# Graph-attention layer: each head's context is stored by ScalarE's queue in place of SyncE's

## The reference

```python
q, k, v = (split_heads(x @ w + b) for each of wq, wk, wv)
scores = einsum("bhqd,bhkd->bhqk", q, k) * dh ** -0.5 + adj[:, None]
ctx = einsum("bhij,bhjd->bhid", softmax(scores), v)      # to [b, n, 384]
x1 = rmsnorm(x + ctx @ wo + bo, alpha1, gamma1)
ff = silu(x1 @ w1 + b1) @ w2 + b2
x2 = rmsnorm(x1 + ff, alpha2, gamma2)
out = layernorm(x + x2)
```

## Time and profile before

| | |
|---|---|
| median of 3 runs | 1932.65 us (1932.32 to 1933.24) |
| the profiled execution, its own time | 1933.91 us |
| its span in the trace | 1932.1 us |
| mean granted TensorE clock | 0.993 of full speed |
| PE busy | 1893.6 us, 98% |
| DVE busy | 1332.8 us, 69% |
| ACT busy | 1141.9 us, 59% |
| POOL busy | 1127.9 us, 58% |
| attention phase | to about 1008 us of the span |
| one batch of it in the loop | 60.2 us |

### The profile page before, as it was taken

How to read it: one execution, slowest core, us unless ns; L and a number is a source line. 1 busy time by engine, 2 the same in 40 slices (tenths; PEclk the granted TensorE clock), 3 DMA queues, 4 the chain that set the end, 5 groups by cost and what they waited for, 6 DMA issues and landing times. The chain is left out here.

```text
span 1932.1 us, 39573 instructions
## 1 busy us (share of the span) xinstructions
PE 1893.6 (98%) x10336; PEld 1608.8 (83%) x10336; DVE 1332.8 (69%) x2579; ACT 1141.9 (59%) x2056; POOL 1127.9 (58%) x1739
## 2 busy tenths in 40 slices
PE   6999999999999999999989999999999999999998
PEld 5777777777877777777768999999999999999997
DVE  5777777777777777777876666656656655666645
ACT  3777777777787777777765444334444334444432
POOL 3655445654456544555667566667665766655643
PEclk9999999999999999999989999999999999999999
DMA  5545545555444554565533222112222112222001
GB/s 173 152 142 152 160 124 142 143 151 160 123 143 142 151 158 125 146 176 152 154 115 125 88 87 84 50 43 83 87 87 87 54 41 79 87 87 87 28 31 41
DMA packets 118732, 214.36 MB, mean 111 GB/s; under 512 B 19489, under 2 KB 47905, under 8 KB 116769
## 3 DMA queue, kind: packets, MB, share of 16 engines
q1 hardware_dynamic: 118688, 213.87, 36.3%
HBM read 108.93 MB, written 41.94 MB: 78 GB/s over the span
## 5 line engine op out<-in xcount | busy, mean ns | idle before, releaser
L982 DVE TENSOR_TENSOR pT_lo<-ps_t,pT_hi 128x512 fp32r<-128x512 f32 x512 | 348.9, 687 | 104.1 <-ACT pT_hi L780 102.9
L780 ACT ACTIVATE pT_hi<-ps_t 128x512 fp32r<-128x512 f32 x512 | 303.1, 596 | 153.4 <-PE ps_t L1221 145.1
L773 ACT ACTIVATE probs<-probs,neg_max 128x512 f32<-128x512 f32 x512 | 357.0, 721 | 34.5 <-DVE neg_max L975 33.4
L975 DVE CUSTOM_DVE_ANT_0 probs<-ps_s,adj_s 128x512 f32<-128x512 f32 x448 | 294.3, 683 | 58.8 <-issue 27.3
L1221 PE MATMUL ps_t<-ident,probs 128*128 128x128 f32 x2048 | 314.2, 277 | 12.3 <-DVE pT_lo L982 9.6
L1221 PEld LDWEIGHTS ps_t<-ident,probs 128*128 128x128 f32 x2048 | 243.1, 141 | 97.4 <-issue 40.5
L1715 DVE TENSOR_TENSOR h_lo<-hidden,h_hi 128x512 fp32r<-128x512 f32 x192 | 170.2, 887 | 172.4 <-ACT h_hi L1625 172.2
L651 POOL CAST tails<-k_wide 16x512 fp32r<-16x512 f32 x384 | 233.4, 608 | 50.6
L647 POOL CAST k_wide<-k_wide 32x512 fp32r<-32x512 f32 x128 | 78.2, 611 | 315.2 <-DMA k_wide<-weights_hi 291.5
L1814 PE MATMUL ps_y<-w_hi,h_hi 128*128 128x384 f32 x768 | 258.2, 336 | 0.0
L1814 PE MATMUL ps_y<-w_hi,h_lo 128*128 128x384 f32 x768 | 257.0, 335 | 0.0
(11 more groups left out here) (114 smaller groups left out, 3963.2 us busy)
## 6 DMA issues: line engine op xcount, KB each, us to landing
ctx_dram<-ctx_stage SPq DMA_DIRECT2D x128, 224.0 KB
ctx_raw<-ctx_dram SPq DMA_DIRECT2D x15, 1792.0 KB, 7.3
q_wide<-weights_lo SPq DMA_DIRECT2D x192, 96.0 KB, 2.3
k_wide<-weights_hi SPq DMA_DIRECT2D x192, 96.0 KB, 2.4
adj_first<-in_adj SPq DMA_DIRECT2D x32, 512.0 KB, 6.5
adj_s<-in_adj SPq DMA_DIRECT2D x32, 512.0 KB, 6.4
rows<-in_xT SPq DMA_DIRECT2D x16, 768.0 KB, 4.9
rows<-in_x SPq DMA_DIRECT2D x16, 768.0 KB, 6.2
```

The costliest lines, as they stand in the source:

```text
L773: nc.scalar.activation(probs[:, at, :], probs[:, at, :], ACT.Exp, scale=-1.0, bias=neg_max[:, at:at + 1]).then_inc(exp_done, 1)
L780: nc.scalar.activation(pT_hi[:, h % 2, qt, :, :], ps_t[qt % 2][:, :].rearrange("p (k i) -> p k i", k=TT), ACT.Copy)\
L975: nc.vector.tensor_tensor_reduce(out=probs[:, at, :], in0=ps_s[qt][:, :], in1=rows, scale=-1.0, scalar=BIG, op0=ALU.add, op1=ALU.min, accu ...
L982: nc.vector.tensor_tensor(pT_lo[:, h % 2, qt, :, :].rearrange("p k i -> p (k i)"), ps_t[qt % 2][:, :], pT_hi[:, h % 2, qt, :, :].rearrange ...
```

## The change

`store_context` is called by ACT, right behind the staging copy of the same head, and no longer by SP. It waits for `ctx_staged` as before, which now is a wait of ACT for its own copy. All eight calls in SP's batch, and the two for heads 6 and 7 of the last batch, are gone. One wait is new on POOL: `last_batch` first waits until every projection of q and k is computed, before it writes W1 over the projection weights.

```diff
-    def store_context(self, sp, ctx_dram, b, h):
-        sp.wait_ge(self.ctx_staged, H * b + h + 1)
-        sp.dma_start(ctx_dram[b, h * ROWS:(h + 1) * ROWS, :, :].rearrange("r k n -> k r n"),
+    def store_context(self, act, ctx_dram, b, h):
+        act.wait_ge(self.ctx_staged, H * b + h + 1)
+        act.dma_start(ctx_dram[b, h * ROWS:(h + 1) * ROWS, :, :].rearrange("r k n -> k r n"),
                      self.ctx_stage[0:V_COLS, h % 2, :]).then_inc(self.ctx_stored[h % 2], DMA)
@@ SP, batch(b)
-                if not first:
-                    shared.store_context(sp, ctx_dram, b - 1, 6)
...
-                shared.store_context(sp, ctx_dram, b, 0)
...
                 stack_next("q", 1)
-                shared.store_context(sp, ctx_dram, b, 4)
 
                 if not last:
                     load_adj_pair(b + 1, 0)
                     load_adj_pair(b + 1, 1)
                 else:
                     seam(6)
-                shared.store_context(sp, ctx_dram, b, 5)
                 stack_next("k", 1)
@@ POOL, last_batch()
+                pool.wait_ge(proj_ready, 2 * KT * B)
                 split_w1(0)
@@ ACT, stage_context(b, h)
                 nc.scalar.activation(ctx_stage[0:V_COLS, h % 2, :], ps_g[bank][0:V_COLS, :], ACT.Copy)\
                   .then_inc(ctx_staged, 1)
+                shared.store_context(act, ctx_dram, b, h)
@@ SP, feed-forward phase
-            shared.store_context(sp, ctx_dram, LAST, H - 1)
```

More of the change, by code:

```diff
@@ L538, in batch @@
                     load_xT(b + 1)
-                if not first:
-                    shared.store_context(sp, ctx_dram, b - 1, 7)
                 if not last:
@@ L557, in batch @@
                     seam(2)
-                shared.store_context(sp, ctx_dram, b, 0)
                 if last:
                     seam(3)
-                shared.store_context(sp, ctx_dram, b, 1)
                 if last_but_two:
                     load_first_context(1)
-                shared.store_context(sp, ctx_dram, b, 2)
                 if last:
@@ L575, in batch @@
                     shared.load_x1_rows(sp, x, 0)
-                shared.store_context(sp, ctx_dram, b, 3)
                 if last_but_two:
@@ L619, in _ @@
             batch(LAST, last=True)
-            shared.store_context(sp, ctx_dram, LAST, 6)
         @block.gpsimd
```

## The result

| | before | after |
|---|---|---|
| median, us (range) | 1932.95 (1932.32 to 1933.69, 4 runs) | 1970.63 (1969.46 to 1971.53, 4 runs) |
| profiled execution: span, us | 1932.1 | 1967.7 |
| one batch in the middle, us | 60.21 | 62.45 |

The ratio is 1.0194, with a 95% interval from 1.0179 to 1.0209. The kernel became slower by 37.7 us, and 17.7 were forecast (1950.4 against 1932.65): the sign was right, the range of 1935 to 1972 just held it, and the loss is more than twice the forecast one.

What follows compares the result with a forecast made beforehand. PE was taken as the bound, busy 59.83 of 60 us per batch; 15 × (0.57 at head 2 + 0.46 at head 5) + 2.2 in batch 15 = 17.7 us, so 1932.65 becomes 1950.4 us, range 1935 to 1972.

Steps and rivals of the forecast that it cites:

- What is removed: SP loses 128 stores, 109 us of its time; PE waits for no DMA, so the gain was put at 0.
- G = 1.1: ACT's delay per store in us: overlap 0.11, wait 0.09, issue 0.85, restart 0.05; ends 0 or about 0.5, and 1.7.
- Head 2: Worst place: ACT's store delays q's high part, then DVE's low part and `pT_lo`; PE stands 0.57 us per batch.
- G = 1.4: A larger ACT delay per store: 1.16 us at head 2, 0.46 + 0.3 at head 5, 32 us in all.
- Head 5: ACT's late `pT_hi` delays DVE's `pT_lo`: PE stands 0.16 us, plus 0.3 waiting for SP's issues, 0.46 per batch.
- The stacking of q starts 1.4 us later: Listed under what costs nothing: q's stacking is delayed, but its readers on POOL stand idle for longer.
- Heads 0, 1, 3, 4, 6, 7: 0: At these heads the nearest `pT_lo` or bank keeps 0.1 to 0.6 us to spare, so the stores cost PE 0.
- Sum: 15 batches of 0.57 + 0.46 us give 15.5, plus 2.2 in batch 15: 17.7 us slower.
- Rival 1: The issue on ACT is hidden or short, under 0.8 us per store, and ACT's idle absorbs it: 1932 to 1936 us; chance 0.15.
- Rival 2: Two issuers hinder each other at every store, about 1.7 us each: 47 us slower, 1980; chance 0.07 together with rival 4.
- Rival 3: Faster: freed SP starts loads and stores sooner, ending at most 7.5 us of PE's waits: 1925 us; chance 0.05.
- Rival 4: PE's standing drops its clock, 2 us lost per batch: 1980 us; chance 0.07 together with rival 2.

Runs made afterwards that it cites:

- the two written-out batches: Batches 13 and 14, written out on ACT outside its loop in a changed kernel that stages q's tile 1 separately in 13 batches; that kernel took 1954.89 us.
- Head 2 alone: The changed kernel with only head 2's store issued by ACT and the other seven of a batch by SP: 1944.62 us, ratio 1.0053.
- head 3's store alone: The changed kernel with only head 3's store issued by ACT and all others by SP: 1951.88 us, ratio 1.0099.
- The spare stores of 7 and 112 KB: All real stores by SP; at head 3 ACT issues an added store of 112 rows into a spare tensor: 1933.57 us with 7 KB, 1935.17 with 112 KB.
- 224 KB from ACT: All real stores by SP; at head 3 ACT issues an added full-size store of 112 rows into a spare tensor: 1949.59 us, ratio 1.0096.
- the kernel with the wait taken away: The changed kernel, all stores on ACT, with q's tile 1 staged in its own place in 13 batches, batches 13 and 14 written out: 1954.89 us.

## Why the prediction was right or wrong

- *What bounds the kernel*: right. PE was full, so each lateness that reached it was lost for good.
- *What is removed, a gain of 0*: right. No kernel here is faster than before, and the one that has SP's stores and the waits alone is the same.
- *G = 1.1*: nearly right. 1.15 to 1.33 measured; the issue is 0.79 (0.85 taken), the wait 0.16 (0.09 taken, the upper end of 0.17 fits), and the start again 0.10 to 0.27 in place of 0.05. All this is in the loop; in the two written-out batches above it is 1.05. (The upper end of 1.7 leaves out the overlap of 0.11 and should be 1.8; nothing rests on it.)
- *Head 2*: the mechanism was right and the term too small: 0.57 forecast, 0.97 at (4,3) to (5,1) in the changed kernel, 1.12 with the steps before them. Head 2 alone gives 0.64 and head 1 adds some 0.4, whose place is (4,3), the transposition from which the prediction took only 0.1. The prediction's own other end, G = 1.4, gave 1.16. With G at 1.33 there, the size fits the error in G, and so do the written-out batches: this is a steep place, at which 0.2 us of G makes some 0.4 us.
- *Head 5*: 0.46 forecast, 0.29 measured. The 0.3 us of waiting for SP did not come: an issue on ACT lasts 0.79 whether SP is issuing, as at head 5 in 15 batches, or not, as at head 2.
- *"The stacking of q starts 1.4 us later; its readers on POOL stand idle for longer than that"*: this is the step that failed: the delay of the stacking was put at nothing. It measured 0.76 to 0.90 us a batch in the loop, 14.0 us in all, and 18.5 us with head 3's store alone. POOL is not the only one that waits for the stacking. ACT itself does, before it overwrites the common staging place with tile 1's high part. ACT's list ahead of the prediction shows this wait at tile 0 already, as `q_stacked2_rest`, and `project_hi` has it for each tile. In the trace of before this wait could hardly be seen, since it was satisfied in all batches but one. What uses it up is mostly not the 1.4 us but something that the prediction had not priced: the stores' data. *Heads 0, 1, 3, 4, 6, 7: 0* fails with it, since I followed what ACT does behind head 3's copy and not what 224 KB do in front of the DMAs that SP issues next.
- *Sum*: 15 × (0.57 + 0.46) + 2.2 = 17.7 forecast. Measured, by the shift at each place: 35.0 in the first 15 batches, 1.8 more up to x1's transpositions. Of 2.24 in batch 7, 1.12 is head 1's and 2's, 0.76 the wait for the landing, 0.29 head 5's. Over the 15 batches heads 1 and 2 make 15.8 us, where 8.6 were forecast, and head 5 3.8, where 6.9 were. So the sum lacked 14.0 us for the missing wait and 7.2 for the size at head 2, and had 3.1 too much at head 5; small steps and batch 15 make up the rest. That the range held the result at all is luck: its upper part was built from G = 1.4 (32 us over before), and not from the missing wait.
- *Rival 1* (hidden or short): no; 0.79 is on ACT's path. *Rival 2* (two issuers): its total was nearer to the truth than mine, for another reason. The spare stores of 7 and 112 KB show two issuers in each other's way by 0.07 and 0.08 us in the group read, and ACT's own issue did not grow. The price fell on SP and on the landing, and came from the bytes. *Rival 3*: no, nothing became faster. *Rival 4*: no, the clock is at its upper level, 1.00 from 70 to 930 us.
- The Trainium skill's "DMA Optimizations" in "Perfetto Trace Analysis", which suggests engines of their own for loads and stores, came out the other way here: 1.9% slower. The Trainium skill's "Issuing engines are not separate DMA queues" in "DMA: Bandwidth & Descriptors" agrees: all that the second issuer brought was SP's time, and the data still met: with 224 KB from ACT in front of it, SP's group landed 1.62 us later. Before, the order of SP's queue had kept them apart: head 3's store stood behind the stackings of q and k (502.76 us in SP's timeline, the last stacking group of q at 496.67).

## What to carry to other kernels

When a DMA is moved to another queue, two orders change: the order of instructions on the new issuer, and the order in which data reach the DMA engines. Look for each later DMA that was behind it and is now beside or ahead of it, and ask who waits for its landing, also for the sake of reusing the source buffer and not only for the data. A wait that is always satisfied has no row in the profile, so read the waits in the code of every engine that has to be on time, and read how much time each has left.

## What was not expected of the hardware

- An issue of 112 rows on ACT took 0.779 to 0.787 us (minimum and median of 128), against a median of 0.853 on SP, where the same DMAs are among other issues. In the loop the activation behind it starts 0.10 to 0.27 us after its end, and the wait for ACT's own copy takes 0.16; in the written-out batch 13 of the kernel with the wait taken away these are 0.05 to 0.12 and 0.03.
- Where issues of both engines coincide, the small one cost SP 0.07 us over three DMAs (1.93 against 1.86). The same issue with 224 KB cost 0.44. With 112 KB it was as with 7 KB, 0.08. So the time that an issue is seen to take can rise with the data that are under way, not only with rows or with the other issuer. It does not have to: in two batches with 224 KB the group took 1.94 and 2.02 and still landed 4.9 behind its start.
- 7, 112 and 224 KB at one place cost 0.2, 2.4 and 16.9 us by the medians, the first two being within what can be told from nothing: a delay of a landing is free until its waiter's time to spare, here 0.39 us, is gone, and what goes beyond it is paid in every batch.
